# A two-layer language-model tower: table-based first projection in one pipeline, preloaded attention units, quartered mask products and a reordered second projection

## Chip, core and metric

One NeuronCore of a Trainium2 chip runs the whole network in one launch. The metric is device microseconds (us) from launch to end. TensorE (PE) multiplies, VectorE (DVE), ScalarE (ACT) and GpSimd (POOL) do the rest, and DMAs are issued from SyncE (SP) and from POOL. Engines run on their own instruction streams and meet at semaphores.

## What is computed

8 sequences of 512 token numbers go through an embedding of rank 32 and two layers. Cut to what the change touches:

```python
x = E1[ids] @ W2.T + b2 + pos                      # 4096 rows of 256
# layer 0 attention, 16 heads of 16, on layernorm(x), no residual here
Q, K, V = (layernorm(x) @ W.T for W in (W_Q, W_K, W_V))
Q, K = rope(Q), rope(K)
attn = softmax(where(causal, Q @ K.T / 4, -inf))
x = x + (attn @ V) @ W_O.T                         # then a mixture of experts
# layer 1: one projection to q and k, k serves as value too; windows 256, 128, ... 4
qk = layernorm(x) @ Wqk + bqk ;  gate = softmax(layernorm(x) @ Wgate + bgate)
# attention inside each head's window, gated, output projection, mixture of experts
```

float32 accuracy is kept by splitting an operand into a high part of a shorter format (fp32r) and the low rest, and adding three products.

## The kernel before

The 4096 rows are 32 tiles of 128 rows, 4 tiles to a sequence ("batch" here). The program is a row of blocks, and at the end of each block all engines meet. Each engine's order of work inside a block is written out by hand.

The first block (`tower`, L2798 to L2815) has only POOL at work: it makes the identity matrix and three mask tables.

`embed` (L108): SP loads token numbers, positions, bias and weights. POOL gathers the 32 tiles of embedding rows (L141), one indirect DMA for each. For every group of 4 tiles PE transposes the rows (L152), ACT copies them to SBUF, PE multiplies them in plain float32 by a block-diagonal W2 (L158), DVE adds position and bias into `res` (L199) and takes mean and variance (L205, L208), ACT takes the root, DVE the reciprocal.

`project_rope` (L278), tile by tile: ACT normalises the row (L355), PE transposes it, ACT and DVE make its high and low parts (L362, L413), and PE makes q and k (6 products of 512 columns, L335) and v (6 of 256, L343). ACT copies q and k out (L383) and v into `va` (L385). POOL multiplies by the sine (L404, two instructions), DVE by the cosine (L438) and adds (L419). PE transposes the result back (L322). ACT and DVE split it into high and low parts (L369, L425), which SP writes to DRAM by batch. SP ends with a wait for these writes (L305).

`attend_pairs` (L1224) works through 32 units (a batch and 4 heads). SP loads q and k parts of a unit from DRAM with 8 DMAs (`scores_in`, L1262), two units ahead; DVE first fills the slot of `ka` with -1 (`minus_rows`, L1460, two instructions of 32 partitions). Per unit there are six query-score and six key-score steps, interleaved over a ring of three PSUM buffers. A step multiplies q by k for two heads at once, on the upper and the lower 64 rows of PE's array (L1321, L1341), and then adds the causal mask of the diagonal 128x128 square by four products (L1327, L1347): two halves of the mask (`part`), each on both row halves. There are 16 such groups of four in a unit, 512 in all. DVE takes maxima of query scores (L1440), ACT exponentials of key scores (L1411), PE multiplies by the values (L1376). POOL splits expert weights meanwhile. `out_ffn_sq` follows.

`project_local` (L446) is the second projection, by batch. In step b PE first transposes the rows of b+1 (`turn_rows`, L534), then makes q and k of b (`products`, L546), the gate logits (L558) and transposes the heads with wide windows (L569). ACT takes the high part of b+1 before the values of b, later the terms, and last normalises b+2 (L587). DVE adds the bias (`rows`, L701), then for b-1 makes the scores of the 10 heads with window 4 (L706 product, L709 sum), takes the low part of b+1 (L690), and does softmax and gates. POOL makes the third term (L660) and the weighted values of b-1 (`near_values`, L666, L671, L673). `attend` follows.

Of the kernel before, what the change touches and what calls it, by code (L numbers as in the profile page):

```python
# [17 lines left out]
P = 128  # L18
# [89 lines left out]
def embed(nc, res, ident, s_got, ids, E1, w2t, b2, pos, ws, rstd, shift):  # L108


    with ExitStack() as ctx:
        k = Kit(nc, ctx, "emb")
        NG = NT // TG
        ids_sb = k.sb("ids", [P, NT], I32)
        rows = k.sb("rows", [P, NT, RANK])
        rowsT = k.sb("rowsT", [P, 2, P])
        w_blk = k.sb("w_blk", [P, TG, D])
        posb = k.sb("posb", [P, TG, D])
        b2b = k.sb("b2b", [P, D])
        stats, mv = k.sb("stats", [P, NT, 6]), k.sb("mv", [P, NT, 2])  # L120
        dev = k.sb("dev", [P, NT])
        psT = k.ps("psT", [P, 2, 512])
        psO = k.ps("psO", [P, 4, 512])
        s = {n: k.sem(n) for n in "ids w pos zero bias T Tc mm res stats mv dev root rstd shift raw hi lo".split()}
        block = ctx.enter_context(nc.Block())

        @block.sync
        def _(sp):
            sp.dma_start(ids_sb[:], ids).then_inc(s["ids"], 16)
            sp.dma_start(posb[:], pos.rearrange("o (t p) d -> p (o t) d", p=P)).then_inc(s["pos"], 16)  # L130
            sp.dma_start(b2b[:], b2.partition_broadcast(P)).then_inc(s["pos"], 16)
            sp.wait_ge(s["zero"], 1)
            for j in range(TG):
                sp.dma_start(w_blk[RANK * j:RANK * (j + 1), j, :], w2t).then_inc(s["w"], 16)
            load_weights(sp, ws, s["raw"])

        @block.gpsimd
        def _(pool):
            pool.wait_ge(s["ids"], 16)
            for t in range(NT):  # L140
                pool.indirect_dma_start(out=rows[:, t, :], out_offset=None, in_=E1,  # L141
                                        in_offset=bass.IndirectOffsetOnAxis(ap=ids_sb[:, t:t + 1], axis=0)
                                        ).then_inc(s_got[t // TG], 16)

        @block.tensor
        def _(pe):
            pe.wait_ge(s["w"], 16 * TG)
            for g in range(NG):
                pe.wait_ge(s_got[g], 16 * TG)
                if g >= 2:  # L150
                    pe.wait_ge(s["Tc"], g - 1)
                pe.transpose(psT[:, g % 2, 0:P], rows[:, TG * g:TG * (g + 1), :], ident[:]).then_inc(s["T"], 1)  # L152
                pe.wait_ge(s["Tc"], g + 1)
                for q in range(2):
                    n = 2 * g + q
                    if n >= 4:
                        pe.wait_ge(s["res"], n - 3)
                    pe.matmul(psO[:, n % 4, :], rowsT[:, g % 2, :], w_blk[:, 2 * q:2 * q + 2, :],  # L158
                              start=True, stop=True).then_inc(s["mm"], 1)

        @block.scalar
        def _(act):
            def root(g):
                act.wait_ge(s["dev"], g + 1)
                at = slice(TG * g, TG * (g + 1))
                act.activation(dev[:, at], dev[:, at], ACT.Sqrt).then_inc(s["root"], 1)

            for g in range(NG):
                act.wait_ge(s["T"], g + 1)
                if g >= 2:  # L170
                    act.wait_ge(s["mm"], 2 * g - 2)
                act.copy(rowsT[:, g % 2, :], psT[:, g % 2, 0:P]).then_inc(s["Tc"], 1)
                if g >= 1:
                    root(g - 1)
                if g == 3:
                    act.wait_ge(s["raw"], 16 * len(ws))
                    for w in ws:
                        act.copy(w["hi"][:], w["raw"][:]).then_inc(s["hi"], 1)
            root(NG - 1)

        @block.vector
        def _(dve):
            def scale(g):
                at = slice(TG * g, TG * (g + 1))
                dve.wait_ge(s["root"], g + 1)
                dve.reciprocal(rstd[:, at], dev[:, at]).then_inc(s["rstd"], 1)
                dve.wait_ge(s["rstd"], g + 1)
                dve.scalar_tensor_tensor(shift[:, at], mv[:, at, 0], -1.0, rstd[:, at], ALU.mult, ALU.mult
                                         ).then_inc(s["shift"], 1)

            dve.memset(w_blk[:], 0.0).then_inc(s["zero"], 1)
            dve.wait_ge(s["pos"], 32)
            dve.tensor_tensor(posb[:], posb[:], b2b[:].unsqueeze(1).to_broadcast([P, TG, D]), ALU.add).then_inc(s["bias"], 1)
            dve.wait_ge(s["bias"], 1)
            for g in range(NG):
                for q in range(2):
                    n = 2 * g + q
# [3 lines left out]
                if g >= 1:  # L201
                    scale(g - 1)
# [2695 lines left out]
```

## Time and profile before

| | us |
|---|---|
| median of 3 runs | 1738.84 (1737.9 to 1739.65) |
| the profiled execution: its time | 1737.24 |
| the profiled execution: span of the trace | 1735.5 |
| PE busy in the span | 1332.6 (77%) |
| DVE, ACT, POOL busy | 873.5, 669.5, 639.0 |
| mean granted PE clock | 0.873 of full |

The span runs from the first to the last instruction. Busy sums over stages with different limits, so the stages have to be looked at one by one. PE has two clock levels, shown as a granted clock of 0.5 and 1.0 (1.2 and 2.4 GHz); a stretch's value is the mean over it.

### The profile page before, as it was taken

Reading aid. Unit: us, or ns where it says so; the run is one execution under the profiler, and the core shown is the slowest. Engines: PE = TensorE matmul, PEld = TensorE weight load, DVE = VectorE, ACT = ScalarE, POOL = GpSimd, SP = SyncE. Lnnn points to the kernel's source line nnn. Section 1 sums busy time; section 2 is a strip of 40 time slices with the busy share of each in tenths; the row PEclk is TensorE's granted clock in tenths of the full one; section 3 lists DMA queues with packets and bytes.
Section 4 is the critical chain, followed back from the end, with each engine's and each line's share of the span. In section 5 each row is a group of like instructions: output and inputs, shape, how many; then the busy total and the mean of one; then the engine's idle time right before and its main releaser. Section 6 shows DMA issues by size and latency. Waiting matters only on the chain. (4 is left out here: it accounts for less than half of the span.)

```text
span 1735.5 us, 31930 instructions
## 1 busy us (share of the span) xinstructions
PE 1332.6 (77%) x10933; PEld 1041.6 (60%) x10934; DVE 873.5 (50%) x1815; ACT 669.5 (39%) x1256; POOL 639.0 (37%) x587
## 2 busy tenths in 40 slices
PE   2699499999997876555189866631897899999997
PEld 1377255555555765544167555521896688888886
DVE  3677667667772783667455355420343233333332
ACT  1377045555554553232045443310342233333332
POOL 7244455555403220256910000077000345444453
PEclk8799589999998996666599988765898899999999
DMA  1044777777620002335344231000002643454331
GB/s 47 4 162 178 219 223 240 240 234 230 205 53 14 1 1 87 117 115 152 88 99 110 48 111 49 13 13 1 24 30 70 222 120 54 120 160 120 82 55 23
DMA packets 122924, 179.46 MB, mean 103 GB/s; under 512 B 26068, under 2 KB 83868, under 8 KB 122820
## 3 DMA queue, kind: packets, MB, share of 16 engines
q1 hardware_dynamic: 94260, 117.18, 22.2%
q0 software_dynamic: 28560, 60.91, 13.6%
q8 instruction: 63, 1.03, 0.3%
q14 instruction: 41, 0.34, 0.1%
HBM read 104.76 MB, written 74.31 MB: 103 GB/s over the span
## 5 line engine op out<-in xcount | busy, mean ns | idle before, releaser
L1440 DVE TENSOR_REDUCE att_top<-att_psS 128x4 f32<-128x512 f32 (+2 forms) x192 | 196.0, 1037 | 82.4 <-PE att_psS L1327 82.3
L1411 ACT ACTIVATE att_prob<-att_psS 128x1024 f32<-128x1024 f32 (+1 forms) x192 | 169.2, 883 | 174.9 <-PE att_psS L1347 174.4
L2597 POOL DMA_INDIRECT out<-ffn1c_y,ffn1c_table x72 | 114.5, 1590 | 179.3 <-DMA out<-ffn1c_y,ffn1c_table 96.8
L2586 POOL DMA_INDIRECT ffn1c_rows<-normed_rows,ffn1c_table x72 | 70.7, 982 | 152.6 <-DVE ffn1c_gate L2758 128.8
L1321 PE MATMUL att_psS<-att_ka,att_qa 48*128 48x384 f32 (+3 forms) x512 | 107.5, 430 | 24.2 <-DMA att_ka<-k_parts 19.7
L2738 DVE TENSOR_TENSOR ffn1c_hid<-ffn1c_psG,ffn1c_sil 128x512 f32<-128x512 f32 x72 | 49.8, 692 | 145.6 <-PE ffn1c_psG L2638 145.6
L1341 PE MATMUL att_psS<-att_qa,att_ka 50*128 50x256 f32 (+3 forms) x512 | 99.6, 401 | 13.8 <-DVE att_top L1440 13.8
L2638 PE MATMUL ffn1c_psG<-ffn1c_w_h,ffn1c_xh 128*128 x288 | 97.3, 419 | 12.6 <-DMA ffn1c_w_l<-experts_lo 6.0
L1321 PEld LDWEIGHTS att_psS<-att_ka,att_qa 48*128 48x128 f32 x512 | 51.9, 199 | 88.9 <-issue 43.2
L1376 PE MATMUL att_psO<-att_prob,values 128*32 128x512 f32 (+3 forms) x1024 | 99.8, 464 | 0.0
L2417 PE MATMUL ffn1b_psG<-ffn1s_xh,ffn1s_w_h 128*128 (+1 forms) x256 | 55.6, 301 | 50.1 <-issue 44.7
L2638 PE MATMUL ffn1c_psG<-ffn1c_w_l,ffn1c_xh 128*128 x288 | 90.7, 397 | 0.0
L2474 DVE TENSOR_TENSOR ffn1b_act_f<-ffn1b_psG,ffn1b_sil 128x256 f32<-128x256 f32 x64 | 27.2, 425 | 125.6 <-remote 63.5
L2638 PE MATMUL ffn1c_psG<-ffn1c_w_h,ffn1c_xl 128*128 x288 | 90.2, 395 | 0.0
L2246 POOL DMA_INDIRECT slots<-ffn1b_entry,ffn1b_sloti x64 | 62.0, 968 | 46.3 <-DVE ffn1b_sloti L2314 27.1
L1327 PE MATMUL att_psS<-m_later,m_half 64*128 64x128 bf16 x1024 | 77.1, 234 | 0.0
L2702 ACT CAST ffn1c_hh<-ffn1c_psH 128x512 fp32r<-128x512 f32 x72 | 42.3, 588 | 86.6 <-PE ffn1c_psH L2649 85.3
L2417 PEld LDWEIGHTS ffn1b_psG<-ffn1s_xh,ffn1s_w_h 128*128 128x128 f32 x256 | 42.7, 205 | 52.0 <-issue 45.2
L1347 PE MATMUL att_psS<-m_sooner,m_half 64*128 64x128 bf16 x1024 | 73.2, 225 | 0.0
L1149 ACT ACTIVATE att_prob<-att_psB 128x384 f32<-128x384 f32 (+4 forms) x112 | 48.9, 472 | 62.4 <-PE att_psB L1076 61.9
L2695 ACT ACTIVATE ffn1c_sil<-ffn1c_psG 128x512 f32<-128x512 f32 x72 | 43.1, 598 | 75.2 <-PE ffn1c_psG L2638 75.2
L1179 DVE TENSOR_REDUCE att_top<-att_psA 128x2 f32<-128x768 f32 (+3 forms) x64 | 51.2, 813 | 40.8 <-PE att_psA L1062 39.9
(385 smaller groups left out, 3593.8 us busy)
## 6 DMA issues: line engine op xcount, KB each, us to landing
prep_raw<-in_w_all POOLq DMA_DIRECT2D x27, 512.0 KB, 4.6
experts_hi<-prep_hi POOLq DMA_DIRECT2D x27, 512.0 KB, 3.8
experts_lo<-prep_lo POOLq DMA_DIRECT2D x27, 512.0 KB, 6.1
ffn1c_w_h<-experts_hi SPq DMA_DIRECT2D x8, 1536.0 KB
ffn1c_w_l<-experts_lo SPq DMA_DIRECT2D x8, 1536.0 KB
qkv_near<-near_keys SPq DMA_DIRECT2D x32, 320.0 KB, 4.2
q_parts<-qkv_part SPq DMA_DIRECT2D x8, 1024.0 KB, 4.0
k_parts<-qkv_part SPq DMA_DIRECT2D x16, 512.0 KB, 5.8
```

What stands on the lines that cost most here:

```text
L1321: pe.matmul(psS[:, bank, g, col:col + cols], qa[r, u % LOADED, q, P * i:P * (i + 1)], ka[r, u % LOADED, q, 0:cols], start=True, stop=True, ...
L1327: mm = pe.matmul(psS[:, bank, g, col + cols - P:col + cols], half[r, part, :], later[r, part, :], start=False, stop=True, tile_position=(6 ...
L1341: pe.matmul(psS[:, bank, g, col:col + cols], ka[r, v % LOADED, q, P * j:P * (j + 1)], qa[r, v % LOADED, q, P * j:S], start=True, stop=True ...
L1347: mm = pe.matmul(psS[:, bank, g, col:col + P], half[r, part, :], sooner[r, part, :], start=False, stop=True, tile_position=(64 * g, 0), sk ...
L1376: mm = pe.matmul(psO[VW * h:VW * h + VW, P * j:S], flat[:, first:first + VW * H:H], prob[:, w % 2, h, START[j]:START[j] + S - P * j], star ...
L1411: act.activation(dst, src, ACT.Exp, scale=0.25).then_inc(s["exp"], 1)
L1440: dve.tensor_reduce(dst, src, AX.X, ALU.max).then_inc(s["max"], 1)
L2246: pool.indirect_dma_start(out=self.dram["table"], in_=self.entry[:, t, n, :], in_offset=None, out_offset=bass.IndirectOffsetOnAxis(ap=self ...
L2417: mm = pe.matmul(psG[:, hb % 2, g, 0:TT], w[:, g, c, cols], x[:, c, bass.ds(i * TT, TT)], start=(q == 0), stop=(q == 5))
L2586: pool.indirect_dma_start(out=rows[:, t.buf, :], out_offset=None, in_=dram["rows"], in_offset=bass.IndirectOffsetOnAxis(ap=table[:, t.valu ...
L2597: pool.indirect_dma_start(out=rows_out, in_=y[:, t.buf, :], in_offset=None, out_offset=bass.IndirectOffsetOnAxis(ap=table[:, t.value:t.val ...
L2638: mm = pe.matmul(psG[:, t.par, g, :], x[:, t.par, P * c:P * (c + 1)], w[:, bass.ds(at, 1), col:col + F1], start=(q == 0), stop=(q == 5))
```

## The change

Four parts.

1. `embed` and `project_rope` and the mask tables' block become one block, `front`. Layernorm is linear apart from the scale, so q, k and v of a row are (row sum through tables) times 1/sigma. Tables are made at the start: W2 less its mean over features times the three weights (`rankX`, `rankQ`), and positions plus bias, less the mean, times the weights (`posX*`, `posQ*`), high and low. A tile is then three products of 512 columns for the row beside v (`psX`) and three for q and k (`psQ`): position high, position low, and the 96 rank terms (high, high, low). The scale 1/sigma goes in when ACT and DVE read PSUM. POOL gathers 20 tiles first and the other 12 inside its loop.
2. `Pairs` holds the buffers `part`, `qa`, `ka`. The first three attention units (`EARLY`) are loaded during `front`; -1 is written by one instruction of 128 partitions a slot. The last wait for the writes to DRAM goes; a unit's load waits for its batch's writes. The second buffer of probabilities lies in `part`.
3. In `attend_pairs` each of the four mask products of a group works on a quarter of PE's array (64 rows by 64 columns), and the second half of the mask streams 64 columns instead of 128.
4. In `project_local` PE does `products(b)` ahead of `turn_rows(b + 1)`, ACT `values(b)` ahead of `high_rows(b + 1)`. DVE adds the bias of two tiles, makes the near product, adds the other two, then makes the sum. `near_values` of the last batch goes from POOL to DVE.

```diff
+class Pairs:
+    LOADED, EARLY, QROWS = 6, 3, 48
...
+    def dve_minus_rows(self, dve, at):
+        dve.memset(self.ka[:, at].bitcast(F32), -1.0).then_inc(self.s_minus, 1)
+
+    def sp_scores_in(self, sp, u):
...
+        sp.wait_ge(self.s_out[b % 2], 16 * 3 * (b // 2 + 1))
+        sp.wait_ge(self.s_minus, min(u, self.LOADED - 1) + 1)
...
+def front(nc, a, res, ident, marks, s_got, pairs, va):
...
+        def _(sp):
...
+            for b in range(B):
...
+                if 1 <= b <= pairs.EARLY:
+                    pairs.sp_scores_in(sp, b - 1)
...
+        def _(pool):
...
+            for t in range(FIRST):
+                gather(t)
+                if t == FIRST // 2 - 1:
+                    terms(0)
+            pool.wait_ge(s["w"], 64)
+            for m in range(NT):
+                if FIRST + m < NT:
+                    gather(FIRST + m)
+                if m % TG == 0 and m // TG + 1 < B:
+                    terms(m // TG + 1)
+                pool.wait_ge(s["qs"], m + 1)
...
+                pool.tensor_tensor(dst, src[:, :, ::-1, :], sn, ALU.mult).then_inc(s["rot2"], 1)
...
+        def _(pe):
+            def position_products(ps, j, w, signal):
+                for c in range(KD):
+                    mm = pe.matmul(ps, posT[:, j, c, :], w[:, c, :], start=(c == 0), stop=(c == KD - 1))
...
+            def sums(ps, m, high, low, table, signal):
+                pe.matmul(ps, one[:], high[:, m % TG, :], start=True, stop=False)
+                pe.matmul(ps, one[:], low[:, m % TG, :], start=False, stop=False)
+                pe.matmul(ps, eS[0:R3, (m // TG) % 2, m % TG, :], table[0:R3, :], start=False, stop=True
...
+            for i in range(NT + 2):
...
+                if i + 1 < NT:
+                    row_and_values(i + 1)
+                if i < NT:
+                    queries_and_keys(i)
...
+                if i % TG == 1 and i // TG + 1 < B:
+                    turn_ranks(i // TG + 1)
+                if i >= 2:
+                    turn_back(i - 2)
...
+        def _(act):
...
+            for i in range(NT + 3):
+                if i < NT:
+                    take_row(i)
...
+                if 1 <= i <= NT:
+                    take_values(i - 1)
+                    take_qk(i - 1)
+                if i % TG == 2 and i // TG + 1 < B:
+                    ranks(i // TG + 1)
...
+                if i < NT:
+                    root(i)
+                if i >= 3:
+                    high_qk(i - 3)
...
+        def _(dve):
...
+            for i in range(NT + 3):
+                if i < NT:
+                    row_stats(i)
...
+                if 1 <= i <= NT:
+                    by_cosine(i - 1)
...
+                if i < NT:
+                    invert(i)
...
+                if 2 <= i <= NT + 1:
+                    turned(i - 2)
+                if i >= 3:
+                    low_qk(i - 3)
...
-                            mm = pe.matmul(psS[:, bank, g, col + cols - P:col + cols], half[r, part, :], later[r, part, :],
-                                           start=False, stop=True, tile_position=(64 * g, 0), skip_group_check=True)
+                            m = slice(64 * part, 64 * part + 64)
+                            mm = pe.matmul(psS[m, bank, g, col + cols - P + 64 * part:col + cols], half[r, part, m],
+                                           later[r, part, 64 * part:], start=False, stop=True,
+                                           tile_position=(64 * g, 64 * part), skip_group_check=True)
...
             for b in range(B):
+                products(b)
                 if b + 1 < B:
                     turn_rows(b + 1)
-                products(b)
...
             for b in range(B):
+                values(b)
                 if b + 1 < B:
                     high_rows(b + 1)
-                values(b)
...
-            near_values(B - 1)
-            pool.wait_ge(s["pv3"], B)
+            pool.wait_ge(s["pv3"], B - 1)
...
             for n in range(B + 1):
                 if n < B:
-                    rows(n)
+                    rows(n, (0, 1))
                 if n >= 1:
                     near_products(n - 1)
+                if n < B:
+                    rows(n, (2, 3))
+                if n >= 1:
+                    near_sums(n - 1)
                 if n + 1 < B:
                     low_rows(n + 1)
...
+            near_values(B - 1)
```

## Rows read from the trace of the kernel before

**Rows 1.** Windows: stage in us; length, busy of each engine; clock, DMA share, GB/s.

```profile
0.00:72.00 72.00, 25.88 (x44) 9.55 (x45) 31.85 (x110) 9.71 (x25) 35.00 (x49) 0.79 0.13 31
72.00:177.00 105.00, 96.00 (x572) 81.08 (x572) 73.83 (x127) 71.88 (x155) 45.51 (x64) 0.98 0.37 141
195.00:240.00 45.00, 38.26 (x342) 22.81 (x342) 34.94 (x43) 9.31 (x11) 23.87 (x21) 0.58 0.80 229
240.00:520.00 280.00, 268.32 (x3619) 157.20 (x3617) 197.31 (x273) 156.32 (x191) 130.08 (x110) 1.00 0.65 203
654.00:854.00 200.00, 104.18 (x512) 89.31 (x512) 113.41 (x178) 55.83 (x115) 92.72 (x38) 0.64 0.36 110
```

**Rows 2.** Embedding: the gathers (min/median/max ns), a plain product, a stall of DVE.

```profile
L141 POOL DMA_INDIRECT emb_rows<-in_E,emb_ids x32: 943/947/1146, 7.2 to 46.2; - x32
L158 PE MATMUL emb_psO<-emb_w_blk,emb_rowsT 128*128 128x512 f32 x32 | 22.5, 841 | 17.6 <-issue 11.6 <-ACT emb_rowsT L172 6.1
41.26 0.18 DVE L211 TENSOR_SCALAR emb_dev<-emb_mv 128x4 f32<-128x4 f32 x1 [4.72 <-remote]
```

**Rows 3.** First projection: groups (busy us, mean ns, idle before), then one instruction's period.

```profile
L425 DVE TENSOR_TENSOR qkv_part<-qkv_psR,qkv_part 128x512 fp32r<-128x512 f32 x32 | 22.1, 692 | 24.8 <-ACT qkv_part L369 24.8
L205 DVE BATCH_NORM_STATS2 emb_stats<-m_res 128x6 f32<-128x256 f32 x32 | 11.2, 412 | 0.0
L383 ACT COPY qkv_qk<-qkv_psQ 128x512 f32<-128x512 f32 x32 | 18.8, 587 | 12.2 <-PE qkv_psQ L335 12.2
L355 ACT ACTIVATE qkv_xn<-m_res,first_shift,first_rstd 128x256 f32<-128x256 f32 x32 | 19.2, 603 | 0.7 <-PEq L111 0.7
L404 POOL TENSOR_TENSOR qkv_rot<-qkv_qk,qkv_sin 128x256 f32<-128x256 f32 x64 | 45.5, 731 | 57.7 <-ACT qkv_qk L383 56.7 <-DVE qkv_qkr L419 1.0
...
85.67 0.62 PE L335 MATMUL qkv_psQ<-first_w_qk_lo,qkv_xTh 128*128 128x512 f32 x2
...
86.13 0.61 PE L335 MATMUL qkv_psQ<-first_w_qk_hi,qkv_xTl 128*128 128x512 f32 x2
...
88.83 0.62 PE L335 MATMUL qkv_psQ<-first_w_qk_lo,qkv_xTh 128*128 128x512 f32 x2
```

**Rows 4.** Timeline from the projection's last instruction to the attention's first.

```profile
176.06 0.69 DVE L425 TENSOR_TENSOR qkv_part<-qkv_psR,qkv_part 128x512 fp32r<-128x512 f32 x1 [1.37 <-ACT qkv_part L369]
...
195.12 0.47 PE L1321 MATMUL att_psS<-att_ka,att_qa 48*128 48x128 f32 x2 [19.71 <-DMA att_ka<-k_parts]
```

**Rows 5.** The fill of slots of ka, grouped by line.

```profile
L1462 DVE MEMSET att_ka<- 32x1024 f32 x12 | 10.9, 912 | 10.5 <-PEq L280 7.5 <-issue 2.9
```

**Rows 6.** Timeline of PE inside a unit at full clock, and its waits from 240 to 520.

```profile
302.15 0.29 PE L1347 MATMUL att_psS<-m_sooner,m_half 64*128 64x128 bf16 x4
...
302.24 0.36 PE L1341 MATMUL att_psS<-att_qa,att_ka 50*128 50x256 f32 x2
...
302.45 0.29 PE L1347 MATMUL att_psS<-m_sooner,m_half 64*128 64x128 bf16 x4
...
302.67 1.10 PE L1376 MATMUL att_psO<-att_prob,values 128*32 128x512 f32 x8
...
PE att_psS L1341 <- DVE att_top L1440: 11.7, 27, 0.4
```

**Rows 7.** Second projection: first bias addition of batches 0 and 7, PE's wait, the end.

```profile
666.50 0.69 DVE L701 TENSOR_TENSOR qkv_qkr<-qkv_psQ,qkv_bias 128x512 f32<-128x512 f32 x1 [4.93 <-PE qkv_psQ L546]
...
747.34 1.97 PE L534 MATMUL qkv_psT<-m_ident,qkv_xn 128*128 128x128 f32 x8 [9.72 <-ACT qkv_xn L587]
...
812.05 0.69 DVE L701 TENSOR_TENSOR qkv_qkr<-qkv_psQ,qkv_bias 128x512 f32<-128x512 f32 x1
...
816.48 2.81 DVE L706 TENSOR_TENSOR qkv_prod<-qkv_near,qkv_qkr 128x2560 f32<-128x2560 f32 x1
...
844.33 4.55 POOL L666 TENSOR_TENSOR qkv_pv<-qkv_near,qkv_pw 128x2560 f32<-128x2560 f32 x1
...
851.92 1.53 POOL L673 TENSOR_TENSOR attn<-qkv_pv 128x640 f32<-128x640 f32 x1
```

More of the change, by code:

```diff
@@ L290, in project_rope @@
+        psE = k.ps("psE", [P, TG, P])
+        s = {n: k.sem(n) for n in (
+            "ids w2 pos w ident marks w2c made copied rankh rankl bias p_stats posc Pv posh posl Pq Pqh Pql "
+            "cath catl E eS X xs stats mv root rstd Q vs qs rot1 rot2 rot3 R h l").split()}
         block = ctx.enter_context(nc.Block())
@@ new lines, in _ @@
+            pe.wait_ge(s["copied"], 2)
+            pe.wait_ge(s["w"], 64)
+            for n, w, cols in ((1, w_v, D), (0, w_qk, 2 * D)):
+                for c in range(KD):
+                    mm = pe.matmul(psX[0:R3, n, 0:cols], w2T[:, c, :], w[:, c, :], start=(c == 0), stop=(c == KD - 1))
+                mm.then_inc(s["made"], 1)
+            pe.wait_ge(s["copied"], 3)
+            for j in range(2):
+                position_products(psQ[:, 2, D * j:D * (j + 1)], j, w_v, s["Pv"])
+            turn_ranks(0)
@@ L389, in _ @@
[L389 to L405 removed]
+            act.wait_ge(s["ident"], 3)
@@ new lines, in _ @@
+            act.activation(dev[:, 0:1], eps[:], ACT.Sqrt)
+            act.copy(one[:], ident[:]).then_inc(s["copied"], 1)
+            act.wait_ge(s["w2"], 48)
+            act.copy(rankX[0:R3, 0:D], w2s[0:R3, :]).then_inc(s["rankh"], 1)
+            act.wait_ge(s["made"], 1)
+            act.copy(w2T[:].rearrange("p c r -> p (c r)"), psR[:, 0, 0:KD * R3]).then_inc(s["copied"], 1)
+            for n in range(2):
+                act.wait_ge(s["made"], 2 + n)
+                act.copy(posT[:, 2 * n:2 * n + 2].rearrange("p j c n -> p (j c n)"), psQ[:, n, :]).then_inc(s["copied"], 1)
@@ L691, in low_rows, with rows @@
                                       ).then_inc(s["xTl"], 1)
-            def rows(b):
+            def rows(b, tiles):
                 if b >= 2:
@@ L697, in rows @@
                     dve.wait_ge(s["vs"], TG * (b - 1))
-                for i in range(TG):
+                for i in tiles:
                     m = TG * b + i
@@ L1400, in exps @@
                 bank = place["B", v, n] % RING
+                if n == 0 and v == 1:
+                    for m in range(2):
+                        act.wait_ge(pairs.s_out[m], 16 * 3 * (B // 2))
                 if n == 0 and v >= 2:
```

549 lines of the change are left out of this document (274 added, 275 removed).

## Prediction, made before the changed kernel was timed

> **What bounds the kernel now.** I read the windows by stage first, because a busy share over the whole span mixes stages. In the first projection PE is busy 96 of 105 us at a clock of 0.98: PE sets the pace, though DVE (73.8) and ACT (71.9) are not far behind. In the attention from 240 to 520 PE is busy 268 of 280 us at full clock; DVE has 197. In the embedding and in the second projection no engine is full: PE has 25.9 of 72 and 104 of 200 us, at clocks of 0.79 and 0.64 [rows 1]. There the groups and waits say who is late. The embedding is paced by POOL's gathers, one in (46.2 - 7.2)/31 = 1.26 us, and by stalls of DVE whose releaser the profile can't name, one of them 4.7 us [rows 2]. Between the projection and the attention 195.1 - 176.8 = 18.4 us pass in which PE does nothing: the writes land, the engines meet, and the first unit is read back [rows 4]. In the second projection a batch takes (812.05 - 666.50)/7 = 20.8 us, and in one of them PE stands 9.7 us until ACT has normalised the next rows, which ACT does last in its step [rows 7].
>
> **Part 1 and 2, up to the attention's first product** (195.1 now). Per tile PE had 18 wide products and 6 transposes; two 512-column products take 86.13 - 85.67 = 0.46, and a tile's period is 88.83 - 85.67 = 3.16 us [rows 3]. Now six products of 512 columns (6 x 0.23 = 1.4) and, by the same rate, about 0.5 of transposes: 1.9 us at full clock, 3.8 at half. PE stops being the bound.
>
> DVE per tile: statistics 0.41 [rows 3], two small operations (aggregate, reciprocal) at 0.18 as the small one in [rows 2], and three operations on 512 elements at 0.69: 0.41 + 0.36 + 2.08 = 2.85 us. One of the three multiplies from PSUM into PSUM, a form without a row; I give it the 0.69 of its neighbours. Consecutive ones can overlap a little: 2.5 is the floor. ACT: row 0.37 (by elements, below the 0.59 of a 512 copy), values with a scale 0.60 as the scaled L355, q and k 0.59 to 0.82 (0.23 more for the scale), high part 0.59, root 0.2, a quarter of a 0.59 copy: 2.5 to 2.7. So DVE sets about 2.85, ACT is just under it. POOL has the sine in one instruction of the same 512 elements (2 x 0.73 = 1.46) [rows 3].
>
> POOL sets the pace at first, since the gathers went onto the path of the loop. The mask tables no longer come first, so I put the first gather at 3 instead of 7.2. Twenty gathers (25 us) and the first terms (1.2) end at 29. Each of the next 12 tiles has a gather, a sine and a quarter of the terms: 1.26 + 1.46 + 0.3 = 3.0, so tile 12 is reached at 65. Behind this the table preparation is hidden: positions and means on DVE to about 13, then some 13 us of plain float32 products on PE (0.84 for 512 columns in one instruction of the pair, which mixes both clocks [rows 2]), most of them before tile 2; even at half clock they end near 38, as POOL is at tile 3. Then 20 tiles x 2.85 = 57: 122. The last tile's low part is a step later, SP issues three writes (2 us) and the engines meet: 128. I add 4 for stalls of the kind in [rows 2], since gathers run again beside the loop: 132. Saved: 195.1 - 132 = 63 us. If DVE runs at 2.5 and nothing stalls it is 121 (-74); if PE's clock drops to half for much of the loop (3.8 a tile) about 145 (-50).
>
> The loads of the three early units are 24 DMA issues on SP, 4 us a unit, between the writes of batches that are 11 us apart; behind them in SP's queue stand only the next batch's writes, and these have two buffers. The wait for the batch's writes is new in front of them; it blocks SP for the landing of the writes and nobody else. Units 3 to 5 are loaded where they were.
>
> **The attention's start.** DVE had 12 fills of 0.91 us [rows 5], two in each of the first four units' steps. Three fills of whole slots now lie in `front`, where DVE waits for its inputs anyway, and three remain. The ramp runs at a clock of 0.58, DVE busy 35 of 45 us [rows 1]: I take 5 us off (0 to 9).
>
> **Part 3, the mask products.** 512 groups of four. Today the group at 302.15 is followed by a product of the same layout (64 rows, 128 columns) after 0.09 us. The group at 302.45 is followed by the values' products, which use another layout (128 rows, 32 columns), after 0.22 [rows 6]: a change of layout costs 0.13 beyond the same group. The quarter products are a third layout (64 by 64) between products of the second, so each group would be entered and left by a change. On the way in I charge nothing: from the product at 302.24 to the masks at 302.45 pass 0.21 us, of which its 256 columns fill 0.11 at the rate of [rows 3], so 0.1 is lost there already. On the way out 0.13 is added. The four products run side by side instead of in two waves of 128 columns: 0.05 saved. Net +0.08 us a group, 16 a unit, +1.3 us on a unit. PE waits little (11.7 us for DVE's maxima in 280 [rows 6]), but around the maxima of steps 1 to 3, when DVE also handles the last unit's maxima, four or five groups lie beside DVE's work. I let 11 of 16 count: 0.08 x 11 x 32 = +29 us. The upper end is all groups at 0.1 with the smaller weights loaded uncovered: +50. The lower end is the 0.05 without any cost: 0.05 x 512 = -26.
>
> The page "TensorEngine Tiling (Array Packing)" of the Trainium skill, Key Properties, says that changing the tiling mode drains the array while changing only the tile does not; the trace agrees with it in its 0.22 against 0.09. The same section says that tiles work in parallel, and its overview promises up to four times; by that promise alone the groups would get shorter and this part would be a gain.
>
> **Part 4, the second projection.** PE's 9.7 us wait goes, since `products(b)` needs only the low part of b, made a step earlier. What is late next is DVE: 113.4 us in the stage over 8 batches are 14.2 a batch [rows 1]. PE's own work is 104/8 = 13 us at a mean clock of 0.64, near 10 at full, and POOL's 92.7/8 = 11.6 is below DVE too. The split of `rows` lets PE go on while DVE does the 2.81 us near product [rows 7]. Gate logits and transposes of PE still leave gaps, so the clock will stay mixed; and the near keys, written and read back after the last bias addition, arrive just when DVE wants them. I take 15.0 instead of 20.8: 7 x 5.8 = 41 us. The first batch starts 2 us sooner, as PE no longer waits for the second batch's rows. At the end POOL's last values took 844.33 to 853.45, 9.1 us, in three instructions; on DVE the first costs 2.81 like L706 [rows 7] and the others by size 1.4 and 0.7: 4.9, but it must wait for POOL's values of batch 6. I take 3 off. Sum 46 us saved. Bounds: 14.2 a batch gives 52, 18 a batch (clock low, keys late) gives 25.
>
> **Sum.** On the profiled execution of 1737.2 us (span 1735.5): -63 - 5 + 29 - 46 = -85, so 1652. The median of the runs, 1738.8, lies 1.6 above the profiled one: 1654. The later stages are not touched.
>
> **Rivals.**
> - *The quarters cost no change of layout* (64x64 counts as the same mode as 64x128). For it: two row halves already run side by side. Against: every other change of form in this stage costs its 0.13. Then part 3 gives 0.05 on 11 of 16 groups, -18 us: 1654 - 29 - 18 = 1607.
> - *The clock or the stalls hold the two pipelined stages back.* PE has less to do per tile (1.9 of 2.85), and the second projection shows what a gappy PE gets: 0.64. Against: at half clock PE would be full, as in the first projection where it got 0.98 [rows 1]. Then `front` ends at 145 and the batch takes 18: -50 - 5 + 29 - 25 gives 1688.
> - *Slower than before: PE loses its full clock in the attention.* If quarter products and drains make PE look idle, the 280 us at clock 1.00 run like the ramp at 0.58. Each us of PE work then takes up to twice as long, of which DVE's slack of 83 us hides nothing, PE being the bound: some +200 us, 1654 + 200 = 1854. It decides from about +85 us, that is if over a third of the attention runs at half clock. Against: products of the same length remain between the groups, and PE stays over 90% busy.
>
> **How the numbers follow.** Forecast 0.60, no cost of layout 0.22, held back 0.14, lost clock 0.03; 0.01 for a change that cancels out. The forecast's own range is 1630 to 1680. The range of all reaches down to just under the first rival and up past the second: 1603 to 1695. Below 0.2% (3.5 us) this kernel's measurement can't tell a difference; faster 0.96, same 0.01, slower 0.03.
>
> **What would show each step.** The attention's first product near 132, with POOL's instructions dense up to about 65 and DVE over 90% busy after it. A tile period near 2.85, and near 3.0 while gathers run. In the attention, a mask group followed by its next product after 0.15 us or more instead of 0.09, and a unit of 11 to 11.5 us instead of 10.3; at 0.05 the first rival holds. In the second projection a period near 15 us with PE's wait for ACT gone and DVE without long gaps. I am wrong in the main if the unit gets shorter, or if `front` is bound by PE or by waits for gathers past tile 12.

## The result: slower, by the lost full clock

The changed kernel takes 1877.8 us (median of 4 runs, 1865.5 to 1879.5) against 1739.2 for the kernel before: 1.078 times as long, with a 95% interval from 1.073 to 1.084. The forecast was 1654. Single executions of the kernel before, 3 of the 24 that ran beside the kernels here, took 1852 to 1935 us (mean clock 0.771 and 0.757 in the two of them for which it is on record); the ratios leave them out, but they matter below.

The page of the changed kernel: span, busy time, and for PE the busy share and the granted clock in 40 slices of the span.

```profile
span 1877.8 us, 31400 instructions
...
PE 1585.5 (84%) x10719; PEld 1084.2 (58%) x10720; DVE 868.0 (46%) x1797; ACT 665.4 (35%) x1260; POOL 631.5 (34%) x569
...
PE   6879999999999998887855996763199699999997
...
PEclk9975555555555555996867998786599799999999
```

PE's busy time grew by 253 us though it has fewer instructions (10719 instead of 10933). The row of clocks shows where: thirteen slices in a row stand at 5, and in the same slices PE's busy share stands at 9, once at 8. The windows of the new front, the attention's ramp, the attention and the second projection (columns as in [rows 1]):

```profile
40.00:120.00 80.00, 67.20 (x338) 47.59 (x336) 76.34 (x186) 65.78 (x162) 58.54 (x62) 0.99 0.68 216
124.00:160.00 36.00, 33.58 (x235) 16.20 (x234) 26.54 (x32) 5.68 (x6) 23.44 (x20) 0.50 0.83 255
160.00:740.00 580.00, 580.00 (x3995) 252.73 (x3993) 219.86 (x289) 179.33 (x217) 136.66 (x116) 0.50 0.34 102
862.00:961.00 99.00, 89.42 (x454) 74.63 (x453) 86.89 (x144) 44.08 (x94) 55.95 (x20) 0.79 0.58 173
```

In [rows 1] the attention had PE busy 268 of 280 us at clock 1.00. Now it is busy 580 of 580 us at 0.50. DVE has 220 in 580, so nothing but PE sets the pace. Stage by stage, from the starts of the first instructions in the two traces:

| | before | after | difference | forecast |
|---|---|---|---|---|
| to the attention's first product | 195.1 | 123.7 | -71.4 | -63 |
| attention | 351.4 | 621.7 | +270.3 | +24 |
| output projection and first experts | 107.7 | 106.4 | -1.3 | 0 |
| second projection and its attention | 339.8 | 283.9 | -55.9 | -46 |
| all that follows | 741.6 | 742.1 | +0.5 | 0 |
| span | 1735.5 | 1877.8 | +142.3 | -85 |

**The front.** Groups of DVE, POOL and ACT between 40 and 120 us (columns as in [rows 3]), then one tile's DVE operations, POOL's first sine and the attention's first product.

```profile
L290 POOL TENSOR_TENSOR front_rot<-front_qk,front_sin 128x512 f32<-128x512 f32 x31 | 40.5, 1309 | 19.2 <-ACT front_qk L432 19.0
L508 DVE SCALAR_TENSOR_TENSOR front_psQ<-front_psQ,front_rstd,front_cos 128x512 f32<-128x512 f32 x31 | 22.6, 730 | 0.2 <-ACT front_qk L432 0.2
L432 ACT ACTIVATE front_qk<-front_psQ,front_rstd 128x512 f32<-128x512 f32 x31 | 21.6, 696 | 0.0
```

```profile
38.60 1.31 POOL L290 TENSOR_TENSOR front_rot<-front_qk,front_sin 128x512 f32<-128x512 f32 x1 [7.77 <-ACT front_qk L432]
...
89.68 0.73 DVE L508 SCALAR_TENSOR_TENSOR front_psQ<-front_psQ,front_rstd,front_cos 128x512 f32<-128x512 f32 x1
90.31 0.15 DVE L502 RECIPROCAL front_rstd<-front_dev 128x1 f32<-128x1 f32 x1
90.38 0.67 DVE L515 TENSOR_TENSOR front_qkr<-front_psQ,front_rot 128x512 f32<-128x512 f32 x1
90.97 0.68 DVE L521 TENSOR_TENSOR pairs_part<-front_psR,pairs_part 128x512 fp32r<-128x512 f32 x1
91.57 0.42 DVE L496 BATCH_NORM_STATS2 front_stats<-m_res 128x6 f32<-128x256 f32 x1
92.02 0.18 DVE L498 BATCH_NORM_AGGREGATE front_mv<-front_stats 128x2 f32<-128x6 f32 x1
92.12 0.73 DVE L508 SCALAR_TENSOR_TENSOR front_psQ<-front_psQ,front_rstd,front_cos 128x512 f32<-128x512 f32 x1
...
123.74 0.48 PE L1452 MATMUL att_psS<-pairs_ka,pairs_qa 48*128 48x128 f32 x2 [4.02 <-PEq L198]
```

DVE is the bound, as forecast (76.3 of 80 us). Its six durations add up to 0.73 + 0.15 + 0.67 + 0.68 + 0.42 + 0.18 = 2.83 us, but the next tile starts after 92.12 - 89.68 = 2.44: five of the six begin 0.08 to 0.1 us before the one ahead has ended.

**The attention.** PE's timeline inside a unit of the changed kernel, all at half clock:

```profile
399.57 0.79 PE L1474 MATMUL att_psS<-pairs_qa,pairs_ka 50*128 50x512 f32 x2
400.29 0.32 PE L1481 MATMUL att_psS<-m_sooner,m_half 64*64 64x64 bf16 x4
...
401.45 0.69 PE L1452 MATMUL att_psS<-pairs_ka,pairs_qa 48*128 48x384 f32 x2
402.07 0.32 PE L1459 MATMUL att_psS<-m_later,m_half 64*64 64x128 bf16 x4
402.32 0.69 PE L1474 MATMUL att_psS<-pairs_qa,pairs_ka 50*128 50x384 f32 x2
```

A group of mask products starts 400.29 - 399.57 = 0.72 us after a 512-column product and is followed after 402.32 - 402.07 = 0.25. A unit takes 19.3 us, where it took 10.3 at full clock.

**The second projection.** DVE's first bias addition of batches 0 and 7 and the near product, which answer to [rows 7]; then what PE waits for in the stage and DVE's wait for the near keys (total us, times, longest).

```profile
862.67 0.69 DVE L826 TENSOR_TENSOR qkv_qkr<-qkv_psQ,qkv_bias 128x512 f32<-128x512 f32 x1 [3.19 <-PE qkv_psQ L672]
...
961.18 0.69 DVE L826 TENSOR_TENSOR qkv_qkr<-qkv_psQ,qkv_bias 128x512 f32<-128x512 f32 x1
...
962.56 3.12 DVE L831 TENSOR_TENSOR qkv_prod<-qkv_near,qkv_qkr 128x2560 f32<-128x2560 f32 x1
```

```profile
PE qkv_psQ L672 <- DVE qkv_xTl L815: 7.8, 6, 2.1
...
DVE qkv_prod L831 <- DMA qkv_near<-near_keys: 4.1, 4, 2.3
```

(961.18 - 862.67)/7 = 14.07 us a batch instead of 20.8. PE's waits of nearly 10 us for ACT are gone. From the second batch on DVE is busy 13.4 to 13.6 us of each.

### The profile page after: what moved, and what is told of

Read it like the earlier page. It is cut to its first block and busy times, and to the rows that moved or that the text cites. A ratio compares the mean times of both kernels' runs of the same rounds, so it can differ in the third digit from the quotient of the medians.

```text
span 1877.8 us, 31400 instructions
## 1 busy us (share of the span) xinstructions
PE 1585.5 (84%) x10719; PEld 1084.2 (58%) x10720; DVE 868.0 (46%) x1797; ACT 665.4 (35%) x1260; POOL 631.5 (34%) x569
## 5 line engine op out<-in xcount | busy, mean ns | idle before, releaser
L1452 PE MATMUL att_psS<-pairs_ka,pairs_qa 48*128 48x384 f32 (+3 forms) x512 | 162.4, 631 | 6.4 <-PEq L198 4.0
L1549 ACT ACTIVATE att_prob<-att_psS 128x1024 f32<-128x1024 f32 (+1 forms) x96 | 84.7, 882 | 228.1 <-PE att_psS L1481 228.0
L1474 PE MATMUL att_psS<-pairs_qa,pairs_ka 50*128 50x256 f32 (+3 forms) x512 | 162.4, 631 | 0.0
L1452 PEld LDWEIGHTS att_psS<-pairs_ka,pairs_qa 48*128 48x128 f32 x512 | 73.6, 284 | 144.4 <-ACT att_prob L1549 46.7
L1549 ACT ACTIVATE pairs_part<-att_psS 128x1024 f32<-128x1024 f32 (+1 forms) x96 | 84.7, 883 | 203.1 <-PE att_psS L1481 202.9
L1474 PEld LDWEIGHTS att_psS<-pairs_qa,pairs_ka 50*128 50x128 f32 x512 | 73.8, 284 | 40.3 <-ACT pairs_part L1549 5.2
L1511 PE MATMUL att_psO<-att_prob,values 128*32 128x128 f32 (+3 forms) x512 | 83.5, 745 | 0.0
L1511 PE MATMUL att_psO<-pairs_part,values 128*32 128x128 f32 (+3 forms) x512 | 82.9, 745 | 0.0
L1481 PE MATMUL att_psS<-m_sooner,m_half 64*64 64x64 bf16 (+1 forms) x1024 | 82.4, 285 | 0.0
L1459 PE MATMUL att_psS<-m_later,m_half 64*64 64x128 bf16 (+1 forms) x1024 | 80.9, 285 | 0.0
```

Of the source, the lines that this page charges most:

```text
L1452: pe.matmul(psS[:, bank, g, col:col + cols], qa[r, u % LOADED, q, P * i:P * (i + 1)], ka[r, u % LOADED, q, 0:cols], start=True, stop=True, ...
L1459: mm = pe.matmul(psS[m, bank, g, col + cols - P + 64 * part:col + cols], half[r, part, m], later[r, part, 64 * part:], start=False, stop=True,
L1474: pe.matmul(psS[:, bank, g, col:col + cols], ka[r, v % LOADED, q, P * j:P * (j + 1)], qa[r, v % LOADED, q, P * j:S], start=True, stop=True ...
L1481: mm = pe.matmul(psS[m, bank, g, col:col + 64 + 64 * part], half[r, part, m], sooner[r, part, 0:64 + 64 * part], start=False, stop=True, t ...
L1511: mm = pe.matmul(psO[VW * h:VW * h + VW, P * j:S], flat[:, first:first + VW * H:H], prob[w % 2][:, h, START[j]:START[j] + S - P * j], star ...
L1549: act.activation(dst, src, ACT.Exp, scale=0.25).then_inc(s["exp"], 1)
```

## Experiments

All are compared with the kernel before on the same chip. Its median was 1653 and 1659 us on two of the chips and 1739 and 1740 on others. Most of this is one late stage that no kernel here touches: it takes about 165 us on the former and 237 on the latter, whatever the kernel. The times in us that were expected of `e1`, `e2`, `e3` and `e5` were reckoned from 1739 and 1879; these four ran where the kernel before takes 1653, so 86 us come off them.

**The changed kernel with the masks of before** (`e1`):

```diff
-mm = pe.matmul(psS[m, ..., col + cols - P + 64 * part:col + cols], half[r, part, m],
-               later[r, part, 64 * part:], ..., tile_position=(64 * g, 64 * part))
+mm = pe.matmul(psS[:, ..., col + cols - P:col + cols], half[r, part, :], later[r, part, :],
+               ..., tile_position=(64 * g, 0))
```

(the same for `sooner`.)

> The changed kernel with the mask products of before (64 rows by 128 columns, two waves of 128 columns); everything else of the change stays. Theory L (the layout of the quarter products keeps PE at its lower clock): PE rises to full clock some 20 to 40 us into the attention, a unit takes 10.3 us again, and the attention lasts about 345 instead of 621 us: 1879 - 276 = about 1603. Rival S (the clock is lost because of how the attention now starts: a pause of a few us after a projection with less work for PE): the granted clock stays at 0.50 in the attention, only the changes of layout go (0.19 us a group at half clock, 512 groups): about 1780.

Measured: 1530.4 us where before is 1653.3, ratio 0.925 [0.923, 0.928]. Its window in the attention, and PE there:

```profile
160.00:430.00 270.00, 258.79 (x3502) 152.36 (x3500) 189.62 (x262) 149.95 (x183) 131.46 (x112) 1.00 0.68 210
```

```profile
213.45 0.48 PE L1472 MATMUL att_psS<-pairs_qa,pairs_ka 50*128 50x512 f32 x2
213.77 0.29 PE L1478 MATMUL att_psS<-m_sooner,m_half 64*128 64x128 bf16 x4
...
214.81 0.29 PE L1458 MATMUL att_psS<-m_later,m_half 64*128 64x128 bf16 x4
214.91 0.37 PE L1452 MATMUL att_psS<-pairs_ka,pairs_qa 48*128 48x256 f32 x2
```

Theory L holds: the clock is 1.00 and a unit 10.3 us, and 1603 - 86 = 1517 was expected. So parts 1, 2 and 4 are a gain of 7.5%, and part 3 alone turns it into a loss.

**Only part 3, in the kernel before** (`e2`, the same edit the other way round).

> The kernel before with only the mask products changed to quarters. Theory L: the attention never gets its full clock, as in the changed kernel: 32 units of 19.4 us instead of 349 us in all, about 2010. Rival S: the clock rises at about 232 as in the kernel before, and the layout changes cost what was predicted: about 1768.

Measured: 1926.1 us in one execution, where before is 1653.3; theory L said 2010 - 86 = 1924.

```profile
230.00:770.00 540.00, 540.00 (x3722) 236.64 (x3715) 213.97 (x280) 163.89 (x200) 129.55 (x109) 0.50 0.34 105
```

So the clock is halved without the pipeline and the preloading too. One execution alone can't show that the quarters did it, since one of seven of the kernel before took 1852 us on this chip. But this one is another 74 us longer, and its units take 19.3 us as in the changed kernel.

**The second half streams 64 columns, but on 64 by 128** (`e3`): as `e1` with `later[r, part, 64 * part:]` and `sooner[r, part, 0:64 + 64 * part]` kept.

> The changed kernel with mask products of 64 rows by 128 columns, but the second half of the mask streams 64 columns instead of 128 (what the change also did). Theory L (it is the layout): full clock as with whole-width masks, and 0.027 us less a group, 512 groups, two thirds on the path: 5 to 14 us below the kernel with whole-width masks of 128 columns, about 1594. Rival C (it is the smaller number of streamed columns, not the layout, that keeps the clock low): clock 0.50 in the attention, about 1770.

Measured: ratio 0.923 [0.918, 0.928], units of 10.1 us.

```profile
160.00:430.00 270.00, 256.92 (x3563) 152.81 (x3561) 193.28 (x267) 152.63 (x188) 132.69 (x112) 1.00 0.70 213
```

It is not the fewer columns.

**Quarters from unit 8 on** (`e5`): `if u < 8:` the masks of before, `else:` the quarters, and the same with `v` for the key scores.

> The changed kernel, with whole-width masks for units 0 to 7 and quarters from unit 8 on. It asks whether quarters take a full clock away or only keep it from rising. Theory L1 (they take it away): the clock rises during the first units and falls to 0.50 within some 10 us of unit 8; about 1603 + 24 x 9 = 1820. Theory L2 (they only keep it from rising): the clock stays at 1.00 to the end of the attention, a mask group with the next product takes 0.15 to 0.18 instead of 0.09 us, a unit 11 to 12 us: about 1630. Rival S: 0.50 from the first unit, about 1860.

Measured: 1726.9 us where before is 1653.3. Windows before unit 8, just after it, and later:

```profile
150.00:191.00 41.00, 39.26 (x530) 22.95 (x528) 28.97 (x40) 23.00 (x28) 27.37 (x24) 1.00 0.87 273
191.00:237.00 46.00, 45.51 (x534) 24.32 (x532) 29.48 (x40) 23.09 (x28) 23.92 (x21) 1.00 0.69 215
253.00:640.00 387.00, 387.00 (x2664) 168.86 (x2662) 148.46 (x196) 119.87 (x145) 80.89 (x68) 0.50 0.31 93
```

Unit 8 starts at 191, the key scores change over at 225, and at 243 a full clock that was held falls and stays down to the attention's end. That is theory L1, though 52 us after unit 8 and not 10 (1820 - 86 = 1734 was expected), and in the one execution that was made. Before the fall the trace shows quarters at full clock, and so their price without the clock: the one unit with both kinds takes 236.8 - 224.8 = 12.0 us instead of 10.3.

```profile
209.06 0.50 PE L1452 MATMUL att_psS<-pairs_ka,pairs_qa 48*128 48x512 f32 x2
209.50 0.24 PE L1463 MATMUL att_psS<-m_later,m_half 64*64 64x128 bf16 x4
209.67 0.39 PE L1478 MATMUL att_psS<-pairs_qa,pairs_ka 50*128 50x256 f32 x2
```

From a 512-column product to the masks pass 209.50 - 209.06 = 0.44 us (0.43 in the median), where `e1` has 213.77 - 213.45 = 0.32 before key masks (the median; before query masks, as here, it is 0.34). From the masks to the next product it is 0.17 against 0.10 where nothing else holds PE up. So a query group on quarters costs about 0.09 on the way in and 0.08 on the way out, 0.17 in all.

**128 columns streamed, but on quarters** (`e6`): `later[r, part, :]` and `sooner[r, part, :]` in the quarters' products.

> The changed kernel with mask products on quarters (64 rows by 64 columns of the array), but both halves of the mask stream 128 columns. Theory L (the 64x64 layout itself takes the full clock away, whatever it streams): the attention again runs at a granted clock of 0.5 with units of about 19.4 us, and the time is 1.08 to 1.11 times the kernel before on the same chip (about 1800 where that is 1653). Rival C (the quarter products take the clock away because they stream fewer columns): the clock comes back to 1.0 in the first 50 us of the attention, units take about 12.3 us, and the ratio is near 0.965 (1530 + 2 x 32 = 1595).

Measured: ratio 1.082 [1.078, 1.085]; units of 19.4 us.

```profile
160.00:700.00 540.00, 540.00 (x3712) 235.90 (x3710) 214.92 (x280) 161.18 (x195) 134.95 (x113) 0.50 0.35 107
```

Theory L holds.

**Only part 1 of each group on quarters** (`e7`): `if part == 0:` the masks of before, `else:` the quarters.

> The changed kernel in which part 0 of each mask group is multiplied on 64 rows by 128 columns as before, and only part 1 on quarters; so every group is entered without a change of layout, changes once in the middle and once at its end. Theory L: the same number of changes of layout per unit as in the changed kernel, and so the clock stays at 0.5 in the attention, units of 19 to 20 us, ratio 1.08 to 1.11. Rival H (the clock is lost only when all four products of a group are on quarters, since half of the quarters' products then leaves half of the array idle): the clock is 1.0 from the attention's first 50 us on, units about 12.5 us, ratio near 0.965.

Measured: ratio 1.105 [1.098, 1.113]; units of 21.0 us, the longest of all.

```profile
165.00:740.00 575.00, 575.00 (x3658) 292.06 (x3650) 212.02 (x277) 159.93 (x194) 131.04 (x112) 0.50 0.33 99
```

Theory L holds in the clock and the ratio; the unit is 1 us longer than it said. Half of the quarters, with a change inside the group, is no better than all of them.

**Quarters in 2 of a unit's 16 groups** (`e8`): quarters only in `query_scores` for `n == 0`.

> The changed kernel with quarters only in the two mask groups of the first query step of a unit (2 of 16 groups), the other 14 on 64 rows by 128 columns. Theory D (the dose decides: few changes of layout leave the clock at full): 1.0 in the attention, units 10.3 + 2 x 0.17 = 10.6 us, ratio 0.925 to 0.935 (about 1535 where before is 1653). Rival A (any quarter product in a unit takes the clock away): attention at 0.5, units of 16.5 to 17 us, ratio above 1.03.

Measured: ratio 0.934 [0.928, 0.941]; units of 10.66 us.

```profile
160.00:450.00 290.00, 278.36 (x3624) 160.51 (x3620) 196.43 (x272) 156.21 (x191) 136.66 (x116) 1.00 0.66 202
```

Theory D holds, and (10.66 - 10.29)/2 = 0.18 us a group agrees with the 0.17 above.

**No mask products** (`e4`): both loops over `part` taken out, so the causal mask is missing.

> The changed kernel without any mask products in the layer-0 attention: it leaves the causal mask out. Sizes what the mask groups cost at full clock. Theory L: without quarters nothing takes the clock away; it is 1.0 from about 150 us on, the 16 groups of a unit give back 0.1 to 0.12 us each, units are 8.4 to 8.8 us (DVE has about 7.2 us of work in one), and the time is about 1475 where before is 1653 (ratio 0.89). Rival W (with less work PE waits for DVE and ACT within the unit and its clock falls): mixed clock, units above 10.3 us, ratio 0.93 or more.

Measured: ratio 0.922 [0.917, 0.927].

```profile
160.00:430.00 270.00, 248.37 (x1804) 117.21 (x1806) 189.55 (x261) 150.52 (x183) 133.20 (x112) 0.80 0.67 212
```

My 1475 (0.89) failed. Units take 10.2 us, as with masks: the time that the masks leave free is lost again to a clock that goes up and down (mean 0.80) and to waits: from 160 to 430 us PE's weight loads wait 96 us for DVE and ACT, against 32 in `e1`. The mechanism of rival W showed, its size did not. A cheaper mask group can thus bring little here (the trimmed one brought 0.2 us a unit).

**Quarters in the key scores only** (`e9`), **in the query scores only** (`e10`).

> The changed kernel with quarters only in the 8 mask groups of the key scores of a unit; the 8 of the query scores on 64 rows by 128 columns. With 2 of 16 groups on quarters the full clock was granted, with 16 it was not. Theory D (the clock falls once enough of a unit's groups are on quarters; 8 are not enough, as the first units with query quarters alone still ran at 1.0): clock 1.0 from about 150 us on, units of 10.3 + 8 x 0.15 = 11.5 us at most, ratio 0.945 to 0.955 of the kernel before. Rival E (8 are enough): attention at 0.5, units of 17.5 to 18 us, ratio 1.05 to 1.07.

> The mirror of the last: quarters only in the 8 mask groups of the query scores. Theory D: clock 1.0, units of 11.3 us (202.1 - 190.8 = 11.3 us was a unit's period at full clock where only the query groups were on quarters), attention 346 + 32 x 1.0 = 378 us, ratio 0.945 to 0.95. Rival E: the run that changed over after unit 7 lost the clock because of them, only later; then the attention is at 0.5 with units of 17.5 to 18 us and the ratio is 1.05 to 1.07.

Measured: 1.049 [1.045, 1.053] and 0.952 [0.949, 0.954]. The first kernel's window, then the second's ramp and attention:

```profile
160.00:650.00 490.00, 490.00 (x3676) 242.45 (x3672) 210.98 (x278) 160.76 (x195) 134.76 (x113) 0.50 0.41 118
```

```profile
125.00:195.00 70.00, 66.88 (x483) 32.60 (x481) 41.26 (x52) 16.27 (x19) 35.58 (x30) 0.50 0.71 210
198.00:490.00 292.00, 287.68 (x3428) 156.05 (x3430) 189.39 (x259) 148.61 (x181) 124.06 (x104) 1.00 0.61 181
```

Theory D failed for the key scores: as many groups, but the clock that fell at 116 comes back only at 656, when the last query scores are done. With query quarters it comes back, 78 us after the fall instead of 38 as in `e1` and `e8`, and units take 11.34 us.

**Quarters in units 0 to 7 only** (`e12`).

> The changed kernel with quarters in units 0 to 7 and 64 rows by 128 columns from unit 8 on: does the full clock come back when the quarters end? Theory B (back): the clock is 0.5 to about 270 us and 1.0 within 50 us after unit 8, as in the ramp with row masks; units of 19.3 us and then 10.3 us; the attention takes 346 + 7 x 9 = 410 to 425 us, ratio 0.965 to 0.975. Rival S (sticks: at half clock the attention doesn't get out of it by itself, since the kernel before also has executions that are 190 us longer at a mean clock of 0.77): 0.5 to the attention's end with units of 16.5 us after unit 8, ratio 1.04 to 1.06.

Measured: 0.969 [0.965, 0.972].

```profile
125.00:258.00 133.00, 130.20 (x912) 59.05 (x910) 65.97 (x83) 34.20 (x41) 54.16 (x47) 0.50 0.55 167
310.00:510.00 200.00, 191.83 (x2598) 112.86 (x2596) 140.47 (x195) 112.00 (x137) 88.23 (x74) 1.00 0.62 191
```

Theory B holds, more slowly than written: the clock is back by itself at 309, 69 us after unit 8's start (240) and 15 us after the key scores, which run three units behind, have changed over too (294). Until then units with quarters in the key scores alone take 17.7 us, and one with none 16.3, the last 1 us of it at full clock.

**Key quarters brought in at full clock** (`e14`): as `e9`, with `if v < 8:` the masks of before.

> The changed kernel with 64 x 128 masks in all query groups and in the key groups of units 0 to 7, quarters in the key groups from unit 8 on. Quarters in all key groups left the clock at 0.5 from the ramp to the end. Theory K (they take it away where it is held): 1.0 from about 155 us, back to 0.5 within some 60 us of unit 8, units of 17.7 us after that; the attention takes 500 to 540 us, ratio 1.01 to 1.04. Rival R (they only keep it from coming back once it is lost): 1.0 to the end, units of 11.3 us from unit 8, attention about 346 + 24 x 1.0 = 370 us, ratio 0.935 to 0.945.

Measured: 0.932 [0.928, 0.936]; units of 10.9 us.

```profile
150.00:223.00 73.00, 69.98 (x949) 40.98 (x942) 51.24 (x71) 40.63 (x50) 45.62 (x40) 1.00 0.82 254
223.00:450.00 227.00, 222.58 (x2775) 122.95 (x2772) 150.98 (x210) 120.51 (x146) 94.21 (x79) 1.00 0.59 181
```

Rival R holds. The same order of products runs at half clock where it starts there (`e9`) and at full clock where it starts there (here), so losing the clock looks like one question and getting it back like another. The two kernels ran on different chips, two executions each, and no run rules out that the chip makes the difference.

**A change of layout without quarters** (`e13`): one product on all 128 rows and columns for each head, its table holding both halves of the mask one below the other.

```diff
-for part in range(2):
-    for g in range(2):
-        mm = pe.matmul(psS[m, ...], half[r, part, m], ..., tile_position=(64 * g, 64 * part))
+for g in range(2):
+    mm = pe.matmul(psS[:, ...], half[:, 0, :], later[:, 0, :], ...)
```

> The changed kernel in which each mask group is two products on all 128 rows and 128 columns of the array (both halves of the mask in one product, one for each head) instead of four on quarters. The columns streamed one after another are as many as with 64 x 128 (two waves of 128), but each group is entered and left by a change of layout. Theory M (the changes of layout around the groups take the clock away, whatever the other layout is): attention at 0.5, units of 18 to 20 us, ratio 1.05 to 1.11 of the kernel before. Rival Q (only products on a part of the columns do it): clock 1.0 from the attention's first 80 us on, units of 10.3 + 16 x 0.13 to 0.17 = 12.4 to 13 us, ratio 0.96 to 0.98.

Measured: two executions, 1834 and 1631 us, where before is 1659; the trace is of the first, with units of 20.3 us.

```profile
160.00:730.00 570.00, 570.00 (x2840) 235.68 (x2841) 215.48 (x280) 162.43 (x197) 133.92 (x113) 0.50 0.33 101
```

Neither theory holds as written. The 204 us between the two are the attention at half clock or not, as far as the mean clocks of 0.763 and 0.894 tell. So 16 groups with a change of layout on both sides, without quarters, need not cost the clock. Whether they make its loss likelier stays open: the kernel before has such executions too (3 of 24).

**The candidate again, with `before` at 1740** (`e11`, the same kernel as `e3`).

> The candidate again: the changed kernel with masks on 64 rows by 128 columns, the second half streaming 64 columns. On a chip where the kernel before took 1653 us it took 0.923 of that. If that holds as a saving in us (129) on a chip where the kernel before takes 1739, it is 1610 here (0.926); the front 71 us sooner, the second projection 56, the attention 5 to 10 us shorter. The rival is that the saving is smaller here because the attention loses its full clock in some executions: then single runs lie 190 us higher.

Measured: 1603.5 us (1600.4 to 1627.4) against 1739.8, ratio 0.921 [0.919, 0.924]. It beats the kernel before by 8%, and the changed kernel by 15% if the two ratios, 0.921 and 1.078, are compared.

## Why the prediction was wrong

**The step that failed** is the argument against the rival "slower than before: PE loses its full clock in the attention", given 0.03: "products of the same length remain between the groups, and PE stays over 90% busy". Both halves are true, and neither protects the clock: PE was busy 580 of 580 us at 0.50. So the sum had no term for the clock, and some 220 us went to it. Once the clock is down the same products take longer (a unit without quarters reaches at 15.0 us, in `e12` at half clock, the product that it reaches at 9.1 in `e1`), so the profile shows PE fuller than ever. The rival's time, 1854, is 24 us under the measured 1878. Its place held, and so did PE as the bound that DVE's slack doesn't relieve; that the drains make PE look idle, the condition that it named, no run shows. How near its time comes is partly luck: the clock and part 3 each cost some 23 us more than it had, and the other parts saved about 20 more. The page "TensorE: Matmul & The Clock Gate" of the Trainium skill, Part 1, says that PE's activity is what releases the full clock; read as the profile's busy time, the trace contradicts it for 580 us.

What supports quarters as the cause: with them in all groups, wholly or for one half of the mask, 4 + 2 + 2 + 1 executions (the changed kernel, `e6`, `e7`, `e2`) had a mean clock of at most 0.77 over the whole kernel, and the four that were traced ran the attention at 0.50. With 64 by 128 in the changed kernel, 12 of 12 (`e1`, `e3`, `e11`) had 0.88 or more, and the three traced ones held 1.00. Within an execution the clock fell after they came (`e5`, one execution) and rose after they went (`e12`). What the chip senses is open. It is not the mere presence of the 64 by 64 layout (`e8`, `e10` and `e14` run at full clock with some of it), nor the columns (`e3`, `e6`), nor only how many groups are on quarters (`e9`, `e10`). The runs would fit a loss that gets likelier with the number of stops around the mask groups, but none of them shows that by itself. The kernel before is not safe either: 3 of 24 executions are 187 to 199 us longer, near the +200 of the rival, though no trace shows in which stage. I had those neither in the runs nor in the argument.

**Part 3 at equal clock.** I had +0.08 us a group, 11 of 16 counted, +29 us in all. "On the way in I charge nothing" was wrong: 0.09 is added there, the 0.08 on the way out is less than my 0.13, and the 0.05 for working side by side is contained in these. Over a unit, query quarters cost 11.34 - 10.29 = 1.05 us and not 8 x 0.17 = 1.36: after two of the eight groups PE waits for DVE's maxima anyway, and the next product comes after 0.29 us instead of 0.41 (medians of `e10` and `e1`). Key quarters cost 10.88 - 10.29 = 0.59. Five of the eight key groups are followed by a product that needed a change of layout already, and there the way out gets shorter, 0.18 us (`e14`) instead of 0.22. Together 1.64 x 32 = 52 us, just past the upper end of 50; the one unit of `e5` with both at full clock, 12.0 us, agrees (1.7). The page "TensorEngine Tiling (Array Packing)" of the Trainium skill, Key Properties, has the drain at a change of mode; the runs add that a group is longer on both sides where both neighbours have another layout. The rest of the attention's 621.7 - 346.9 = 275 us against `e1`, some 220, is the clock, by difference.

**The front** was right in kind and 8 us too slow. DVE bounds it, PE's clock is 0.99, so the rival in which clock or stalls hold it back is out. The size off is the 2.85 a tile, a sum of durations; 2.44 was measured, under my floor of 2.5. The loop started later than my sum had it: POOL waited 7.8 us for the first q and k at 38.6, when the 20 gathers had long ended (27.7), so the table preparation and not POOL set the start. Then 12 tiles with gathers took (70.1 - 38.6)/12 = 2.6 us each, not 3.0. The two errors, of opposite sign, left tile 12 at 70 instead of 65. So part of what the 2.85 had too much was cancelled by a start that I had too early.

**The attention's start** gave 351.4 - 346.9 = 4.5 us (`e1` against the kernel before), forecast 5.

**The second projection** gave 55.9 us, forecast 46, 4 past my end of 52. A batch takes 14.07 us instead of my 15.0, at the bound that DVE's work gave (14.2), because the near keys came nearly in time (4.1 us of waits in all) and DVE waited 7.9 us for PE instead of 58.1. That is 47 us of the gain; the start gives 1.5, and the end, with `near_values` on DVE, 7.3 instead of 3.

Without part 3 the sum of my terms is -114 us. Measured: -123 (`e1`), and with the trimmed masks -129 and -136 on two chips (`e3`, `e11`).

## What to carry to other kernels

Where PE is the bound at full clock, changes of layout added all through a stage can put the clock at stake, and that stake (here 220 us) has to be priced beside the 0.1 us stalls themselves; PE was over 90% busy in this stage at 1.00 and at 0.50, so look at the granted clock of the same stage, in several executions before and after. Charge a product in another layout on both its sides. For an engine that works without waits, take the distance between starts, not the sum of durations.

## What the runs showed of the hardware that I had not expected

- The same products run for 490 us at 0.50 or for 227 us at 1.00, and in both traces they go on at the clock at which they begin (`e9`, `e14`, on two chips).
- Taking the mask products off PE (1804 product instructions in 270 us instead of 3502) lowered the mean clock from 1.00 to 0.80 and saved 0.1 us a unit (`e4`, `e1`).
- Half the clock doesn't double the price of the quarters. At half clock a unit reaches its second 128-column key product after 15.0 us with 64 x 128 masks (`e12`) and after 17.2 with quarters (the changed kernel), 2.2 more; at full clock the whole unit is 1.7 longer (`e5`).
- One and the same late stage takes about 165 us on some chips and 237 on others. In the long one PE stands idle for 49 us in two stretches, the longer of 29, for which the profile names no releaser (the changed kernel); the short one has no such stretch (`e1`).
